# A bidirectional selective scan: the reversed parts' output projection and gate projection at other steps of the loop and in other PSUM banks

## What is computed

```
h = layernorm(seq) + pos                       # seq: 2 images x 2304 tokens x 256
xi, z = split(h @ in_proj_w.T)                 # 512 channels each
y_f = branch(xi, z, forward weights)
y_b = branch(xi[:, ::-1], z[:, ::-1], backward weights)[:, ::-1]
out = seq + (y_f + y_b) @ out_proj_w.T

branch: xs = silu(conv4(xi)); proj = xs @ xproj_w.T
        dt = softplus(proj[:16] @ dtproj_w.T + b); Bm, Cm = proj[16:32], proj[32:48]
        per token: state = exp(dt * A) * state + (dt * xs) * Bm    # 512 channels x 16 states
                   y = sum over states of state * Cm, plus xs * D
        result y * silu(z)
```

## Time and profile before

| what | value |
|---|---|
| median of 3 runs | 5890.46 us (5889.35 to 5890.49) |
| the profiled execution's own time | 5906.89 us |
| its span | 5905.1 us |
| the scan loop in it | from 151.0 to 2316 us |
| mean granted TensorE clock | 0.917 of full |

### The profile page before, as it was taken

One profiled execution on the slowest core, in us unless ns is written; L12 is line 12 of the kernel. 1 busy time (PEld: TensorE's weight loads), 2 busy tenths in 40 slices (PEclk: granted clock), 3 DMA queues, 4 the chain that ended last, 5 costly groups with the idle time before them and its releaser, 6 DMA issues. The chain is left out here.

```text
span 5905.1 us, 54130 instructions
## 1 busy us (share of the span) xinstructions
PE 4882.1 (83%) x15186; PEld 2726.7 (46%) x15187; DVE 3428.7 (58%) x4954; ACT 2082.3 (35%) x3362; POOL 2321.0 (39%) x2102
## 2 busy tenths in 40 slices
PE   5877888987778886998997876473999899997797
PEld 3333333433333332554555554452555555555575
DVE  2999999999999997693862323574222200002113
ACT  2655666656666563322321111000222212212123
POOL 3888888888888885011120000182000000002102
PEclk7999999999999999999998888586999999995899
DMA  2444344334443342001000001100001000001233
GB/s 97 134 117 149 126 125 129 117 120 135 126 132 123 120 135 83 29 0 52 28 14 16 5 16 42 26 5 7 23 16 44 19 0 2 0 0 41 72 95 75
DMA packets 221102, 383.47 MB, mean 65 GB/s; under 512 B 35036, under 2 KB 208269, under 8 KB 216037
## 3 DMA queue, kind: packets, MB, share of 16 engines
q1 hardware_dynamic: 206868, 367.49, 19.6%
q0 software_dynamic: 7552, 7.81, 0.8%
q10 hardware_dynamic: 6480, 5.90, 0.4%
HBM read 334.99 MB, written 48.71 MB: 65 GB/s over the span
## 5 line engine op out<-in xcount | busy, mean ns | idle before, releaser
L917 POOL TENSOR_TENSOR DBU<-DU,BB 128x461 f32<-128x461 f32 (+1 forms) x1280 | 1371.4, 1085 | 330.6 <-DVE PS L961 320.1
L592 PE MATMUL PS<-G,ident 128*128 128x461 f32 (+1 forms) x2560 | 1158.3, 580 | 390.0 <-DVE G L972 388.0
L961 DVE TENSOR_TENSOR_SCAN PS<-PS,HC,DBU 128x461 f32<-128x461 f32 (+1 forms) x1024 | 1147.9, 1165 | 5.0 <-ACT PS L768 5.0
L768 ACT ACTIVATE PS<-DT,alog 128x461 f32<-128x461 f32 (+1 forms) x1280 | 825.8, 645 | 817.0 <-DVE PS L961 814.7
L592 PEld LDWEIGHTS PS<-G,ident 128*128 128x128 f32 x2560 | 462.1, 194 | 1051.5 <-DVE G L972 801.8
L972 DVE TENSOR_TENSOR G<-PS,CB 128x461 f32<-128x461 f32 (+1 forms) x1280 | 785.8, 623 | 38.7 <-PE PS L592 38.6
L2717 POOL TENSOR_TENSOR xs<-X 128x384 f32 x12 | 11.7, 991 | 829.7 <-issue 527.9
L2686 DVE TENSOR_TENSOR X<-X,PS 128x768 f32 x12 | 11.4, 954 | 553.5 <-PE PS L2653 553.5
L2581 DVE TENSOR_TENSOR Hg<-Hg,GB 128x384 f32<-128x384 f32 x192 | 106.7, 558 | 372.8 <-ACT Hg L2568 372.8
L2642 PE MATMUL PS<-QT,N 128*128 x864 | 310.3, 486 | 4.9 <-ACTq L2659 4.9
L2653 PE MATMUL PS<-AT,XT 128*128 128x384 f32 x864 | 310.5, 487 | 0.0
(11 more groups left out here) (423 smaller groups left out, 7515.8 us busy)
## 6 DMA issues: line engine op xcount, KB each, us to landing
BB<-proj_dram SPq DMA_DIRECT2D x256, 461.0 KB, 3.9
CB<-proj_dram SPq DMA_DIRECT2D x64, 922.0 KB, 6.1
BB<-proj_dram SPq DMA_DIRECT2D x64, 460.0 KB, 4.6
ew<-in_l_w SPq DMA_DIRECT2D x16, 1024.0 KB, 6.8
CB<-proj_dram SPq DMA_DIRECT2D x16, 920.0 KB, 5.9
GB<-gate_dram SPq DMA_DIRECT2D x12, 768.0 KB, 4.1
w_fc<-in_l_w_fc SPq DMA_DIRECT2D x4, 2048.0 KB, 11.8
XI<-xi_dram SPq DMA_DIRECT2D x8, 928.0 KB
```

What stands on the lines that cost most here:

```text
L592: pe.matmul(PS[:, j, :wide(g)], k.ident[:], G[:, S % 4, :wide(g)], start=False, stop=(n == DS - 1))\
L768: act.activation(DA(S), DT[:, j, :wide(g)], ACT.Exp, scale=w.alog[:, chunk(g)[1], j, n:n + 1]).then_inc(da_done, 1)
L917: pool.tensor_tensor(DBU[:, S % 4, :wide(g)], DU[:, j, :wide(g)], BB[:, 2 * u + n % 2, :wide(g)], ALU.mult).then_inc(dbu_done, 1)
L961: dve.tensor_tensor_scan(flow(HS(S), g), flow(DA(S), g), flow(DBU[:, S % 4, :wide(g)], g), start, ALU.mult, ALU.add).then_inc(h_done, 1)
```

## The change

`out` moves from s = 22, 23, 25, 26 to s = 48, 49, 51, 52, and from banks 2 and 3 to banks 0 and 1; its emptying on ACT moves from s = 33 to s = 55. `z` moves from s = 47, 48, 53, 55 to s = 55, 56, 59, 61, its emptying from s = 52 to 60 to s = 58 to 63, and the sigmoid's last two functions to steps 0 to 3 of the next chunk, with `gate_z` four to two steps later. The convolution moves from s = 10, 12, 15, 18 to s = 11, 13, 16, 19, in every chunk but the last. `xi` moves by some steps only in chunks 8, 9 and 10. Waits follow the banks. No operation is added or removed, and no size changes.

```diff
@@ mamba_chunks
+    def xi_at(g):
+        if g == LATE:
+            return 62, 62, 63, 63
+        return (55, 56, 59, 60) if is_rev(g - 1) else (47, 48, 52, 53)
+
+    def xi_taken(g):
+        return (58, 59, 61, 62) if is_rev(g - 1) else (52, 53, 57, 58)
@@ tensor, xi
                 if j < 2 and h:
                     pe.wait_ge(dt_base, 2 * (h - 1) + 1)
+                    if h >= 2 and rev_before(h - 2):
+                        pe.wait_ge(o_added, rev_before(h - 2))
@@ tensor, z
                 if j < 2:
                     pe.wait_ge(dt_base, 2 * h + 1)
+                    if rev_before(h - 1):
+                        pe.wait_ge(o_added, rev_before(h - 1))
@@ tensor, out
                     if g + 2 < NCH:
-                        pe.wait_ge(cv_exp, JD * (g + 2) + 3 + m)
+                        pe.wait_ge(dt_base, 2 * (g + 2) + 1)
                     elif g + 1 < NCH:
-                        pe.wait_ge(dt_base, 2 * (g + 1) + 2)
+                        pe.wait_ge(y_taken, 2 * (g + 1) + 1)
+                    if rev_before(g):
+                        pe.wait_ge(o_added, rev_before(g))
                     pe.wait_ge(xr_in, 16 * (rev_before(g) + 1))
-                    pe.matmul(PS[:, 2 + m, :wide(g)], k.ident[:], XR[:, m, :wide(g)], start=True, stop=False)
+                    pe.matmul(PS[:, m, :wide(g)], k.ident[:], XR[:, m, :wide(g)], start=True, stop=False)
                 for j in range(2 * half, 2 * half + 2):
-                    mm = pe.matmul(PS[:, 2 + m, :wide(g)], w.w_out[:, j, m * P:(m + 1) * P], Z[:, g % 2, j, :wide(g)],
+                    mm = pe.matmul(PS[:, m, :wide(g)], w.w_out[:, j, m * P:(m + 1) * P], Z[:, g % 2, j, :wide(g)],
@@ tensor, first
                 if p == 0:
                     pe.wait_ge(dt_base, 2 * g + 1)
+                    if g and rev_before(g - 1):
+                        pe.wait_ge(o_added, rev_before(g - 1))
...
-                    if is_rev(g - 1):
-                        pe.wait_ge(o_added, rev_before(g))
@@ tensor, the loop's table
-                    if s == 10:
+                    if s == 11:
                         conv(h, 0)
-                    elif s == 12:
+                    elif s == 13:
                         conv(h, 1)
-                    elif s == 15:
+                    elif s == 16:
                         conv(h, 2)
-                    elif s == 18:
+                    elif s == 19:
                         conv(h, 3)
...
                 if is_rev(g - 1):
-                    if s == 22:
+                    if s == 48:
                         out(g - 1, 0, 0)
-                    elif s == 23:
+                    elif s == 49:
                         out(g - 1, 0, 1)
-                    elif s == 25:
+                    elif s == 51:
                         out(g - 1, 1, 0)
-                    elif s == 26:
+                    elif s == 52:
                         out(g - 1, 1, 1)
...
                 if is_rev(h):
-                    if s == 47:
+                    if s == 55:
                         z(h, 0)
-                    elif s == 48:
+                    elif s == 56:
                         z(h, 1)
-                    elif s == 53:
+                    elif s == 59:
                         z(h, 2)
-                    elif s == 55:
+                    elif s == 61:
                         z(h, 3)
-                if is_fwd(g + 2):
-                    if s == (60 if g == LATE else 47):
-                        xi(g + 2, 0)
-                    elif s == (61 if g == LATE else 48):
-                        xi(g + 2, 1)
-                    elif s == (62 if g == LATE else 52):
-                        xi(g + 2, 2)
-                    elif s == (63 if g == LATE else 53):
-                        xi(g + 2, 3)
+                if is_fwd(g + 2) and s in xi_at(g):
+                    for j in range(JD):
+                        if s == xi_at(g)[j]:
+                            xi(g + 2, j)
@@ scalar
-                act.activation(k.X[:, :, b * L + at:b * L + at + n], PS[:, 2:2 + KC, :n], ACT.Copy).then_inc(o_added, 1)
+                act.activation(k.X[:, :, b * L + at:b * L + at + n], PS[:, 0:KC, :n], ACT.Copy).then_inc(o_added, 1)
...
-                if s == 33 and is_rev(g - 1):
+                if s == 55 and is_rev(g - 1):
                     take_out(g - 1)
...
                 if is_rev(h):
-                    if s == 52:
+                    if s == 58:
                         take_z(h, 0)
-                    elif s == 53:
+                    elif s == 59:
                         exp_z(h, 0)
-                    elif s == 54:
                         take_z(h, 1)
-                    elif s == 55:
+                    elif s == 60:
                         exp_z(h, 1)
-                    elif s == 56:
-                        log_z(h, 0)
-                    elif s == 57:
+                    elif s == 61:
                         take_z(h, 2)
-                    elif s == 58:
+                    elif s == 62:
                         exp_z(h, 2)
-                    elif s == 59:
+                    elif s == 63:
                         take_z(h, 3)
-                    elif s == 60:
                         exp_z(h, 3)
-                    elif s == 61:
-                        sig_z(h, 0)
-                    elif s == 62:
-                        log_z(h, 1)
-                    elif s == 63:
-                        sig_z(h, 1)
...
+                if is_rev(g):
+                    if s == 0:
+                        log_z(g, 0)
+                    elif s == 1:
+                        sig_z(g, 0)
+                    elif s == 2:
+                        log_z(g, 1)
+                    elif s == 3:
+                        sig_z(g, 1)
+                if is_fwd(g + 2) and g != LATE and s in xi_taken(g):
+                    take_xi(g + 2, xi_taken(g).index(s))
@@ gpsimd
-                if is_rev(g) and s in (1, 3, 6, 9):
-                    gate_z(g, (1, 3, 6, 9).index(s))
+                if is_rev(g) and s in (5, 7, 9, 11):
+                    gate_z(g, (5, 7, 9, 11).index(s))
```

More of the change, by code:

```diff
@@ L810, in _ @@
                 if is_rev(h):
-                    if s == 52:
+                    if s == 58:
                         take_z(h, 0)
-                    elif s == 53:
+                    elif s == 59:
                         exp_z(h, 0)
-                    elif s == 54:
                         take_z(h, 1)
-                    elif s == 55:
+                    elif s == 60:
                         exp_z(h, 1)
-                    elif s == 56:
-                        log_z(h, 0)
-                    elif s == 57:
+                    elif s == 61:
                         take_z(h, 2)
-                    elif s == 58:
+                    elif s == 62:
                         exp_z(h, 2)
-                    elif s == 59:
+                    elif s == 63:
                         take_z(h, 3)
-                    elif s == 60:
                         exp_z(h, 3)
-                    elif s == 61:
-                        sig_z(h, 0)
-                    elif s == 62:
-                        log_z(h, 1)
-                    elif s == 63:
-                        sig_z(h, 1)
[L835 to L840, removed]
-                        take_xi(g + 2, 2)
-                    elif s == 58:
-                        take_xi(g + 2, 3)
+                if is_rev(g):
[9 more added lines that the diff above has]
+                    take_xi(g + 2, xi_taken(g).index(s))
                 if g == LATE and s == 63:
```

## The result

The changed kernel takes 5916.49 us (median of 5 runs, 5910.85 to 5921.26) against 5890.46 us (5887.70 to 5900.03) before: ratio 1.0041, interval 1.0028 to 1.0054.

The account below looks back on a forecast made before the run. VectorE was taken to set the scan loop's time. Savings of 27.7 us and additions of 52.5 us gave +25 us, so 5915 us on the median of 5890.46 us; range for 8 in 10: 5894 to 5936 us.

Parts of the forecast that it names:

- (a): Convolution one step later in 19 chunks: waits at steps 16 and 22 go, small ones stay; 21.5 us saved.
- (b): out leaves s = 22 to 26: the eight waits at step 30 go; 6.2 us saved.
- (c): take_out at s = 55 waits for out and delays step 56's scan 3.0 us in nine chunks; 27 us added.
- (d): floor_rest and the z copies at chunk ends, and log_z in step 0, delay decays in nine chunks; 17 us added.
- (e): Chunk 8 besides out: z 3, then xi and their copies, stand ahead of step 0's decay; 3.5 us added.
- (f): Chunks 9 and 10 besides out: floor_rest and the copies of xi 2 and xi 3 delay decays; 5 us added.
- Rival 2: ScalarE's waits in the loop are absorbed and only the gains remain: -27.7 us, 5863 us, faster; chance 0.07.
- rival 3: Only take_out binds and the z copies fit in: 5890 us, no change; chance 0.11.
- Rival 4: The clock falls in TensorE's matmul chains as well: +18 us, 5933 us; chance 0.15.
- The rule against this change: Idling throttles TensorE's clock, so thinner steps 22 to 26 should make xproj slow in more chunks; no size given.

Follow-up runs that it names:

- e5: Kernel before the change with one number changed, take_out on ScalarE at s = 29 instead of s = 33; ratio 1.0047.
- e7: Changed kernel with only ScalarE's copies later (take_out at s = 57, z and xi too, except in chunk 8), TensorE's order untouched; ratio 0.9962.
- e2: Changed kernel with the convolution back at s = 10, 12, 15, 18; ratio 1.0077 against the kernel before.
- e1: Kernel before the change with only the convolution moved, to s = 11, 13, 16, 19; ratio 0.9987.
- e6: e1 with out at s = 24, 25, 27, 28 instead of 22, 23, 25, 26; ratio 0.9955 against the kernel before.
- e3: Changed kernel with take_out on ScalarE at s = 57 instead of s = 55; ratio 1.0024 against the kernel before.
- e4: e3 with the copies and exps of z 2 and z 3 and the sigmoid's last functions later too; ratio 1.0017 against the kernel before.
- e8: Changed kernel with out at s = 46, 47, 49, 50 instead of 48, 49, 51, 52; ratio 1.0015 against the kernel before.

## Why the prediction was right, and where it was off

**The mechanism was right**, in the prediction's own places: waits for decays from 5.2 to 54.9 us ("some 50"), take_out waiting 5.3 us ("some 5"), steps 16, 22 and 30 clear. The waits for TensorE fell further than forecast, to 3.2 us instead of "about 10". e5 and e7 show the mechanism from both sides: the copy's distance alone makes the loss in the old kernel, and the copies' distances alone take it away in the new one.

**(a), convolution: 21.5 us forecast.** A chunk without out gained 1.0 to 1.1 us, 20 us for 19 chunks, and e2's 23.5 us come to the same without the 3 us of its chunks 17 and 18. Its leftovers came out as 0.55 at step 20 and 0.33 to 0.34 at step 25 in the four chunks without a carry, where 1.0 was reckoned for the two together, and as 0.15 at step 25 in some others, where it was 0.3. Of the 26.6 us that I gave to steps 16 and 22, 1.3 us in chunks 7 and 8 belong to the lower clock (last section). What the step didn't say is that alone it would give only 8.2 us (e1), because its gain in chunks with out needs (b).

**(b), out leaves 22 to 26: 6.2 us.** The eight waits are gone. By e1 and e6 it is worth more once the convolution has moved: 1.7 us and more in eight chunks.

**(c), take_out: 27 us.** Measured 2.96 to 3.01 in eight chunks and 3.73 in chunk 10, 27.6 us together.

**(d), floor_rest and z: 17 us.** 0.24 instead of 0.4 for floor_rest, 0.67 for z 2, 0.36 and 0.24 instead of 0.5 and 0.4 for z 3 and log_z: 1.5 us instead of 2.0 in each of five chunks, so 7.5 instead of 10. The four chunks without out have 1.3 to 1.4 each, 5.4 us instead of 7. The sentence that z 0 and z 1 "just fit" is borne out in these four; in the chunks with out it holds only because VectorE is 3 us late there; e3 showed 1.81 us behind z 0 once that is taken away.

**(e), chunk 8: 3.5 us.** 4.74 + 1.14 and 0.68 + 0.24 make 6.8, less 3.36: 3.4 us. **(f): 5 us**; 2.3 and 2.4 measured.

**The sum** was +25 us, and the loop shows +17.6. About 4.5 us are the sizes in (d) and (f). The largest single part is the waits at step 40, which I had let stand: 6.5 us in six chunks before, 0.98 in one after, 5.5 us. Of the same kind are the waits at steps 10 and 11 of chunks 7 and 8 before, 1.7 us, against 0.17 us after. The other way goes what a wait costs beyond its idle time: at the prediction's estimate of 0.09 us, the 58 more waits for decays make about 5 us, which the idle times above leave out. These parts are estimates and don't close to the last 1 or 2 us.

The median of 5916.49 thus lies nearer to the forecast of 5915 than the loop bears out, and that nearness is luck. The other 8.4 us between the medians lie outside the loop, where the kernels are the same and two profiles of one kernel, taken on different chips, differ by 25 us (3743.7 and 3718.7 us before; 3730.0 and 3726.0 after); where in particular they come from was not studied.

**The rivals.** Rival 2 (absorbed, faster) and rival 3 (only take_out binds) fall by the waits. Rival 4, the lower clock in the chain, is not there: the mean granted clock over out is 1.00 in all nine chunks, and out and z in chunk 6 run at 1.71 us for four passes throughout. What spoke for it, 0.97 us at step 16 of chunk 7 against 0.37 in chunk 6, was the lower clock at another place, ahead of the convolution (last section).

**The rule against this change** (the Trainium skill, "TensorE: Matmul & The Clock Gate", Part 1), from which I took that the thinner stretch ahead of the gating would be slow in more chunks, isn't borne out in the way I applied it. The kernels with out at s = 22 to 26 have the wait at step 40 in 6, 7 and 4 chunks (before, e1, e5), those with out at s = 46 to 52 in 1, 1, 7, 4, 4 and 6 (after, e2, e3, e4, e7, e8): which of the two places out has doesn't decide it. The trace does show that the level falls behind an idle stretch; what I had overlooked is that the idle stretch itself can change. Over all 13 profiles xproj met the lower clock in 49 of the 103 cases in which TensorE had stood idle for 2.38 to 2.51 us just before, in none of the 130 forward chunks (1.49 us or less), and in none of the 14 cases with 0.68 us that e6 and its repeat have. That the shorter gap is the cause was not tested by itself.

## What to carry to other kernels

An engine that takes its work in order pays for a copy out of PSUM with everything queued behind it, so set the copy's step by when the matmul will be through, counted with the backlog in front of it, and not by the matmul's own step: for `take_out` three steps were too few, and five and seven cost nothing. When one such wait is removed, look which copy was hidden by it before counting the gain. The shortest loop of this study moves only the convolution by one step and the output projection by two, and leaves copies, gate and banks alone (e6, ratio 0.9955, interval 0.9933 to 0.9976); by its time it can't be told from e7 (0.9962, 0.9946 to 0.9978).

## What the runs showed of the hardware that I had not expected

Behind the gating of y, where TensorE stands idle for 2.4 to 2.5 us, xproj's eight passes take 3.30 us in some chunks and 3.9 to 5.5 us in others. In the changed kernel's chunk 6:

```profile
849.32 1.83 PE L607 MATMUL PS<-G,ident 128*128 128x461 f32 x2 [2.51 <-DVE G L974]
851.08 4.16 PE L524 MATMUL PS<-XS,w_x 128*49 128x461 f32 x8
```

The mean granted clock over these 6 us is 0.79 and over the next 6 us 0.93 of full (the column behind the engines' busy times), so the lower of the two levels, 1.2 GHz, held for part of the time:

```profile
846.00:852.00 6.00, 3.49 (x7) 0.86 (x6) 6.00 (x9) 1.95 (x3) 2.96 (x3) 0.79 0.26 79
852.00:858.00 6.00, 6.00 (x16) 2.24 (x15) 5.02 (x10) 1.95 (x3) 3.44 (x4) 0.93 0.00 0
```

The same happens at the start of some chunks, behind another gap of 2.51 us. The kernel before in chunk 7, steps 5 to 9 (dt, then five sums in one row), and the window behind it:

```profile
909.70 2.91 PE L592 MATMUL PS<-G,ident 128*128 128x461 f32 x4 [2.51 <-DVE G L972]
912.53 3.44 PE L526 MATMUL PS<-PJ,w_dt 17*128 17x461 f32 x4
915.90 6.41 PE L592 MATMUL PS<-G,ident 128*128 128x461 f32 x10
914.00:920.00 6.00, 6.00 (x9) 2.27 (x8) 5.11 (x7) 3.99 (x6) 3.22 (x4) 0.50 0.22 79
```

The granted clock is 0.50, ten passes of sums take 6.41 us, and VectorE waits 0.67 and 0.21 us at steps 10 and 11 and 0.97 us at step 16. In the changed kernel the clock at this place of chunk 7 is 1.00. The lower level by itself costs nothing: in chunk 1 of the kernel before the granted clock over the pair of step 46 is 0.50 as well, and VectorE waits for nothing there.

I had taken it for chance which chunks are hit. In two executions each of two kernels, which reached the loop within 0.2 us of the same moment, the same chunks were hit at step 40, with waits equal to some hundredths of a microsecond; in the two of e6, where the loop began 2.1 us earlier, another one was. A small shift ahead of the loop may thus be enough to move such waits, but this one pair is all that shows it. At step 40 alone they came to between 1 and 8 us of this loop. That comes with every comparison of two orders, and e1, e3, e6 and e8 missed their numbers partly by it.
